# Coupled outputs of four batches taken ahead, x1 parts moved to the coupling's third cycle, and a new order at the last batch

## The reference

```python
xn = layernorm(x)
# attention and feed-forward branch
q, k, v = split(xn @ Wqkv + bqkv); qp, kp = elu(q) + 1, elu(k) + 1
attn = qp @ (kp^T v) / (qp . sum(kp) + eps)
x1 = layer_norm(xn + attn) * g1 + b1
ffn = (silu(x1 @ Wg + bg) * (x1 @ Wu + bu)) @ Wd + bd        # 341 hidden features
s = layer_norm(x1 + ffn) * g2 + b2
# coupling branch
gf = global_net(mean(xn)); out = xn
for _ in range(3):
    tf = sigmoid(gelu(gelu(gelu(out @ w1 + b1) @ w2 + b2) @ w3 + b3) @ w4 + b4)     # one number a token
    out = out + (0.1 + range * 2 * (0.7 * gf + 0.3 * tf - 0.5)) * twist(out)
result = x + s * silu(out)
```

## Time and profile before

| | us |
|---|---|
| median of 3 runs | 187.56 |
| profiled execution, whole | 185.62 |
| its span, first to last instruction | 183.8 |
| TensorE busy (matmul) | 161.3 |
| VectorE busy | 146.4 |
| ScalarE busy | 124.9 |
| GpSimd busy | 107.9 |

### The profile page before, as it was taken

The page is one execution under the profiler, slowest core; times in us unless marked ns, Lnnn a source line. Parts: engine busy times, 40 slices in busy tenths (PEclk is TensorE's granted clock), DMA queues, the critical chain, the costliest instruction groups (busy, mean ns, idle before and its releaser), DMA issues.

```text
span 183.8 us, 3473 instructions
## 1 busy us (share of the span) xinstructions
PE 161.3 (88%) x979; PEld 114.0 (62%) x982; DVE 146.4 (80%) x567; ACT 124.9 (68%) x320; POOL 107.9 (59%) x204
## 2 busy tenths in 40 slices
PE   0289999999999989989969899789999999999920
PEld 0146777777777776446524445448887887888820
DVE  4694789999987988599999940366969889889695
ACT  2227866988979976978856685885576765774430
POOL 0259667879994689950011223139768586595981
PEclk9999999999999999999997999999999999999996
DMA  5980000000000000000000000000001010010113
GB/s 98 312 338 0 0 0 5 0 2 2 0 4 0 2 5 0 0 4 0 0 0 0 2 4 0 2 0 4 2 0 57 0 61 32 27 57 4 59 57 114
DMA packets 3331, 5.75 MB, mean 31 GB/s; under 512 B 496, under 2 KB 1136, under 8 KB 3312
## 3 DMA queue, kind: packets, MB, share of 16 engines
q1 hardware_dynamic: 3312, 5.52, 9.0%
HBM read 3.43 MB, written 2.10 MB: 30 GB/s over the span
## 4 chain that ended last, share of the span: by engine, by line
PE 54%; DVE 21%; POOL 8%; ACT 7%; issue 4%; DMA 3%; SPq 1%; DVEq 0%; ACTq 0%; POOLq 0%
PE bank L1041 11%; DVE r_tok L639 6%; PE bank L1029 6%; PE bank L1030 5%; PE bank L1031 5%; DVE pq L652 5%; PE bank L885 5%; DVE r_tok L642 3%; DMA r_tok<-in_w_first 3%; POOL rstd L231 3%; PE bank L969 3%; PE bank L918 2%; PE bank L919 2%; PE bank L921 2%; PE bank L930 2%
## 5 line engine op out<-in xcount | busy, mean ns | idle before, releaser
L441 ACT ACTIVATE pq<-bank,bffn 128x512 f32<-128x512 f32 (+1 forms) x24 | 16.3, 685 | 16.4 <-PE bank L1031 16.4
L231 POOL TENSOR_TENSOR rstd<-ve,minus_half 128x4 f32<-128x4 f32 (+1 forms) x25 | 24.8, 992 | 2.1
L1041 PE MATMUL bank<-wd,pq 128*128 128x128 f32 x168 | 23.4, 283 | 0.0
L230 POOL TENSOR_SCALAR ve<-mv 128x4 f32<-128x4 f32 (+1 forms) x25 | 5.1, 206 | 30.1 <-DVE nm L539 29.2
L1029 PE MATMUL bank<-x_hi,ffn_hi 128*128 128x512 f32 (+1 forms) x48 | 20.8, 433 | 1.8 <-ACT pq L441 1.3
L676 DVE SCALAR_TENSOR_TENSOR pq<-bank,bffn,pq 128x512 f32<-128x512 f32 (+1 forms) x24 | 17.8, 746 | 5.0 <-ACT pq L441 3.2
L1041 PEld LDWEIGHTS bank<-wd,pq 128*128 128x128 f32 x168 | 21.2, 193 | 0.2
L392 ACT ACTIVATE q_stage<-bank,col 128x512 f32<-128x512 f32 x24 | 16.3, 686 | 6.8 <-PE bank L885 6.0
L1030 PE MATMUL bank<-x_lo,ffn_hi 128*128 128x512 f32 (+1 forms) x48 | 19.0, 396 | 0.0
L1031 PE MATMUL bank<-x_hi,ffn_lo 128*128 128x512 f32 (+1 forms) x48 | 19.0, 395 | 0.0
L921 PE MATMUL bank<-first_hi,xT_lo 128*128 128x512 f32 x32 | 15.4, 482 | 0.0
(11 more groups left out here) (134 smaller groups left out, 463.6 us busy)
## 6 DMA issues: line engine op xcount, KB each, us to landing
x_tok<-in_x SPq DMA_DIRECT2D x8, 256.0 KB, 6.3
out<-pq SPq DMA_DIRECT2D x7, 256.0 KB, 2.0
r_tok<-in_w_ffn SPq DMA_DIRECT2D x1, 341.0 KB, 6.2
r_tok<-in_w_first SPq DMA_DIRECT2D x1, 320.0 KB, 5.3
out<-pq SPq DMA_DIRECT2D x2, 128.0 KB, 1.8
small<-in_w_small SPq DMA_DIRECT2D x1, 242.0 KB, 4.0
row<-in_rows SPq DMA_DIRECT2D x1, 192.0 KB, 5.8
wd<-in_w_down SPq DMA_DIRECT2D x1, 192.0 KB, 6.3
```

Of the source, the lines that this page charges most:

```text
L231: return pool.tensor_tensor(rstd[i][:, b, ts], ve[i][:, b, ts], minus_half[:, ts], ALU.pow)
L1041: last = pe.matmul(dst[:, t * P:(t + 1) * P], hid[b % 2][0:m, c, t * P:(t + 1) * P], wd[0:m, c], start=False, stop=(c == CHUNKS - 1))
```

## The change

- **Coupled outputs.** For batches 0 to 3 (`EARLY`) GpSimd, not ScalarE, computes `a * xn`, in place in SBUF, directly behind the scalars of a pair; VectorE adds `b * twist` from there in slots 10 and 11, ahead of the first hidden product. Batches 4 to 7 stay on ScalarE, with a semaphore of their own, and are spread over the first batches of the feed-forward.
- **Late x1 parts.** Transposition and high part of batches 6 and 7 move from slots 2 and 4 to slots 8 and 9, their low parts on VectorE from slots 1 and 3 to behind the updates of slot 7 and the coupling of slot 8. The multiplications by g1 of these batches move behind all scalars on GpSimd.
- **Third chunk.** Gate and up products of chunk 2 go to banks 1 and 2, which the coupling's layer 2 has left, and wait for no SiLU or hidden product.
- **SiLU of chunk 0** moves ahead of the last tanh on ScalarE.
- **Last batch's order.** The whole down product of batch 6 stands between chunks 22 and 23 on TensorE, and VectorE takes the residual of batch 6 ahead of hidden product 23.

```diff
@@ -34,6 +34,8 @@
 CHUNKS = -(-HID // P)
 CHUNK_ROWS = [min(P, HID - c * P) for c in range(CHUNKS)]
 ACT_NORMS = 5
+EARLY = 4
+X1_SLOTS = {0: 5, 8: 6, 9: 7}
 PAIRS = BATCHES // 2
 CYCLES = 3
 HALVES = ((0, 1), (2, 3))
@@ -180,12 +182,18 @@
         ctx_ready, gf_ps, gf_act, base_ready = sem("ctx_ready"), sem("gf_ps"), sem("gf_act"), sem("base_ready")
         h1_ps, h1_ready, h2_ps, h2_ready = sem("h1_ps"), sem("h1_ready"), sem("h2_ps"), sem("h2_ready")
         h3_ps, h3_ready, z_ps, tt_ready = sem("h3_ps"), sem("h3_ready"), sem("z_ps"), sem("tt_ready")
-        r_ready, s_ready, cpl_ready, ab_ready, ax_ready, o_ready = [
-            sem(n) for n in ("r_ready", "s_ready", "cpl_ready", "ab_ready", "ax_ready", "o_ready")]
+        r_ready, s_ready, cpl_ready, ab_ready, ax_ready, axp_ready, o_ready = [
+            sem(n) for n in ("r_ready", "s_ready", "cpl_ready", "ab_ready", "ax_ready", "axp_ready", "o_ready")]
         gate_ps, up_ps, sg_ready, hid_ready = sem("gate_ps"), sem("up_ps"), sem("sg_ready"), sem("hid_ready")
         down_ps, u2_ready, un_ready = sem("down_ps"), sem("u2_ready"), sem("un_ready")
         g_ready, mn_ready, y_ready = sem("g_ready"), sem("mn_ready"), sem("y_ready")
         y_stored = [sem("y_stored0"), sem("y_stored1")]
+
+        def gate_of(n):
+            return bank[1] if n == 2 else ps_gate[n % 2]
+
+        def up_of(n):
+            return bank[2] if n == 2 else ps_up[n % 2]
         block = ctx.enter_context(nc.Block())
@@ -293,6 +301,13 @@
                 pool.tensor_tensor(a, a1, t1, ALU.subtract)
                 pool.tensor_tensor(b, b1, t0, ALU.add).then_inc(ab_ready, 1)
+            def scale_xn(b):
+
+                pool.wait_ge(ab_ready, b // 2 + 1)
+                pool.wait_ge(tx_ready, b + 1)
+                a = ab[:, b // 2, 2, TILES * (b % 2):TILES * (b % 2) + TILES].unsqueeze(2).to_broadcast([P, TILES, D])
+                pool.tensor_tensor(xn_tok[:, b], xn_tok[:, b], a, ALU.mult).then_inc(ax_ready, 1)
+
             def gate_rows(b):
                 pool.wait_ge(g_ready, b + 1)
@@ -318,12 +333,15 @@
                     norm_x1(b - 2)
                 if 3 <= b < BATCHES + 1:
                     scale_x1(b - 3)
-            for b in (BATCHES - 2, BATCHES - 1):
-                scale_x1(b)
             for j in range(PAIRS):
                 scalars_2(j)
             for j in range(PAIRS):
                 scalars_3(j)
+                if 2 * j < EARLY:
+                    scale_xn(2 * j)
+                    scale_xn(2 * j + 1)
+            for b in (BATCHES - 2, BATCHES - 1):
+                scale_x1(b)
             for b in range(BATCHES):
                 gate_rows(b)
                 if b == BATCHES - 1:
@@ -417,14 +435,14 @@
             def scale_xn(b):
                 act.wait_ge(ab_ready, b // 2 + 1)
-                if b == 0:
+                if b == EARLY:
                     act.wait_ge(tt_ready, SLOTS)
                 else:
                     act.wait_ge(o_ready, b)
                 for t in range(TILES):
                     i = TILES * (b % 2) + t
                     last = act.mul(ps_ax[:, t], xn_tok[:, b, t], ab[:, b // 2, 2, i:i + 1])
-                last.then_inc(ax_ready, 1)
+                last.then_inc(axp_ready, 1)
             def silu_o(b):
                 act.wait_ge(o_ready, b + 1)
@@ -438,7 +456,7 @@
                 if n == 0:
                     act.wait_ge(bffn_ready, 1)
                 m = CHUNK_ROWS[c]
-                act.activation(sg[n % 2][0:m], ps_gate[n % 2][0:m], ACT.Silu,
+                act.activation(sg[n % 2][0:m], gate_of(n)[0:m], ACT.Silu,
                                bias=bffn[0:m, c:c + 1]).then_inc(sg_ready, 1)
             def norm_2(b):
@@ -477,8 +495,8 @@
             global_act(2)
             for s in range(SLOTS - 2):
                 gelu_2(s)
-                if s in (0, 2, 4):
-                    hi_x1(BATCHES - 3 + s // 2)
+                if s in X1_SLOTS:
+                    hi_x1(X1_SLOTS[s])
                 if s >= 1:
                     tanh_z(s - 1)
                 gelu_1(s + 2, (0,))
@@ -490,16 +508,16 @@
             gelu_3(SLOTS - 2)
             tanh_z(SLOTS - 2)
             gelu_3(SLOTS - 1)
+            silu_gate(0)
             tanh_z(SLOTS - 1)
             for b in range(BATCHES + 1):
                 if b < BATCHES:
-                    silu_gate(CHUNKS * b)
-                    if b == 0:
-                        scale_xn(0)
+                    if b >= 1:
+                        silu_gate(CHUNKS * b)
                     silu_gate(CHUNKS * b + 1)
-                    if b + 1 < BATCHES:
-                        scale_xn(b + 1)
                     silu_gate(CHUNKS * b + 2)
+                if EARLY <= b + EARLY < BATCHES:
+                    scale_xn(b + EARLY)
                 if b == 0:
                     silu_o(0)
                 if b >= 2:
@@ -657,11 +675,15 @@
             def o3(b):
                 j = b // 2
-                dve.wait_ge(ax_ready, b + 1)
+                if b < EARLY:
+                    dve.wait_ge(ax_ready, b + 1)
+                else:
+                    dve.wait_ge(axp_ready, b - EARLY + 1)
                 for t in range(TILES):
                     i = TILES * (b % 2) + t
                     last = dve.scalar_tensor_tensor(out=xn_tok[:, b, t], in0=tx_tok[:, b, t],
-                                                    scalar=ab[:, j, 3, i:i + 1], in1=ps_ax[:, t],
+                                                    scalar=ab[:, j, 3, i:i + 1],
+                                                    in1=xn_tok[:, b, t] if b < EARLY else ps_ax[:, t],
                                                     op0=ALU.mult, op1=ALU.add)
                 last.then_inc(o_ready, 1)
@@ -673,7 +695,7 @@
                 dve.wait_ge(sg_ready, n + 1)
                 if b >= 2:
                     dve.wait_ge(down_ps, b - 1)
-                dve.scalar_tensor_tensor(out=hid[b % 2][0:m, c], in0=ps_up[n % 2][0:m],
+                dve.scalar_tensor_tensor(out=hid[b % 2][0:m, c], in0=up_of(n)[0:m],
                                          scalar=bffn[0:m, CHUNKS + c:CHUNKS + c + 1], in1=sg[n % 2][0:m],
                                          op0=ALU.add, op1=ALU.mult).then_inc(hid_ready, 1)
@@ -847,21 +869,26 @@
                     next_r(s)
                 if 2 <= s < PAIRS + 2:
                     minus_s(s - 2)
-                if s in (1, 3):
-                    lo_x1(BATCHES - 2 + s // 2)
+                if s in (7, 8):
+                    lo_x1(s - 1)
+                if s >= SLOTS - 2:
+                    o3(2 * (s - SLOTS + 2))
+                    o3(2 * (s - SLOTS + 2) + 1)
             for b in range(BATCHES):
                 hidden(CHUNKS * b)
                 if b >= 3:
                     finish(b - 3)
-                if b == 0:
-                    o3(0)
                 hidden(CHUNKS * b + 1)
-                if b + 1 < BATCHES:
-                    o3(b + 1)
+                if b + EARLY < BATCHES and b >= 1:
+                    o3(b + EARLY - 1)
+                if b == BATCHES - 1:
+                    residual_2(b - 1)
                 hidden(CHUNKS * b + 2)
-                if b >= 1:
+                if 1 <= b < BATCHES - 1:
                     residual_2(b - 1)
+                if b == BATCHES - EARLY:
+                    o3(BATCHES - 1)
             last = BATCHES - 1
             residual_last(0)
@@ -1019,16 +1046,16 @@
             def gate_up(n, parts=(0, 1)):
                 b, c = divmod(n, CHUNKS)
                 m = CHUNK_ROWS[c]
-                if n >= 2 and 0 in parts:
+                if n >= 3 and 0 in parts:
                     pe.wait_ge(sg_ready, n - 1)
                 for k in parts:
-                    dst, done = ((ps_gate, gate_ps), (ps_up, up_ps))[k]
-                    if k == 1 and n >= 2:
+                    dst, done = ((gate_of(n), gate_ps), (up_of(n), up_ps))[k]
+                    if k == 1 and n >= 3:
                         pe.wait_ge(hid_ready, n - 1)
                     w = slice(k * HID + c * P, k * HID + c * P + m)
-                    pe.matmul(dst[n % 2][0:m], ffn_hi[:, w], x1_hi[:, b], start=True, stop=False)
-                    pe.matmul(dst[n % 2][0:m], ffn_hi[:, w], x1_lo[:, b], start=False, stop=False)
-                    pe.matmul(dst[n % 2][0:m], ffn_lo[:, w], x1_hi[:, b], start=False, stop=True).then_inc(done, 1)
+                    pe.matmul(dst[0:m], ffn_hi[:, w], x1_hi[:, b], start=True, stop=False)
+                    pe.matmul(dst[0:m], ffn_hi[:, w], x1_lo[:, b], start=False, stop=False)
+                    pe.matmul(dst[0:m], ffn_lo[:, w], x1_hi[:, b], start=False, stop=True).then_inc(done, 1)
             def down(b, tiles):
                 pe.wait_ge(hid_ready, CHUNKS * (b + 1))
@@ -1103,8 +1130,8 @@
                 if s == 1:
                     pe.wait_ge(gf_act, 3)
                 layer_2(s)
-                if s in (0, 2, 4):
```

(16 more changed lines are left out.)

## The result

| | before | changed |
|---|---|---|
| median of the runs, us | 187.23 (184.88 to 188.20, 4 runs) | 191.94 (191.62 to 193.08, 4 runs) |
| profiled execution, us | 185.62 | 191.97 |
| its span, us | 183.8 | 190.2 |
| mean granted clock | 0.983 | 0.959 |

The change made the kernel slower: 1.0314 times the time before [1.0245 to 1.0384, the 95% interval], and 4.7 us in the medians; the forecast for the median was 191.4. The two profiled executions are 6.35 us apart, and that splits into four stretches, of which one lies in code that the change does not touch.

What follows compares the result with a forecast made beforehand. TensorE binds from 123 to 173 us, VectorE's update chain before that; +1.1 (early outputs, coupling included), +1.5 (clock), +1.3 (last batch) make +3.9 us, median 191.4, own range 189.8 to 192.9, overall 188.0 to 193.3.

Steps and rivals of the forecast that it cites:

- The coupling: Coupling slots up to layer 1 behind slot 9: of VectorE's 1.8 us lead only 0.09 us is left.
- the wait in slot 9: TensorE in slot 9 stands 1.17 us, its moved transposition of batch 7 waiting for batch 6's low part.
- The early outputs: Feed-forward entry: first hidden product at 121.5 instead of 117.76, first down product at 125.05 instead of 123.95, +1.1 us.
- The hold of batch 3's: Ahead of the first hidden product, GpSimd's g1 multiplications hold batch 3's first two VectorE updates, 1.30 us each instead of 0.27.
- Rival A: Ahead of the first hidden product GpSimd waits, not VectorE; 187.9 to 189.4 us; chance 0.21.
- The clock: Behind TensorE's 4.3 us standing at the fourth up product, the clock falls: +1.5 us, bounds 0 and 2.5.
- The last batch: At the end, batch 5's normalisation behind the last SiLU delays GpSimd's finish and the last stores: +1.3 us.
- Sum: Whole kernel: +1.1 + 1.5 + 1.3 = +3.9 us on the profiled 185.62, giving 189.5; median 191.4.
- B: Faster: VectorE's lead reaches TensorE, placed at slot 9; 185.4, up to 186.8 us; chance 0.18.
- C: Clock falls a second time, behind the 1.17 us standing in slot 9: +1.5 more, 192.9 us; chance 0.07.
- D: Tanh needs its own table: two loads more, 1.28 us each, before slot 11's coupling or second gate; 192.7 to 194; chance 0.03.

Runs made afterwards that it cites:

- hidden-first experiment: Changed kernel with VectorE's updates of batches 2 and 3 moved from ahead of the first hidden product to behind the third: 191.96 us, 1.0287.
- the second execution: Both kernels profiled once more, unchanged: 186.79 us for the kernel before, 192.67 us for the changed kernel.
- the two experiments: Changed kernel with the last batch's old order: 190.41 us, 1.0209; kernel before with only the last batch's new order: 187.94 us, 1.0053.

## Why the prediction was right, and where its terms were off

**The coupling** was right: forecast -0.09, measured -0.20, with the wait in slot 9 at 1.23 us for a forecast 1.17. The experiment that removed it shows it worth 1.27 us.

**The early outputs** were forecast at +1.1, the coupling's gain included, and took 0.62 (0.82 without that gain). The first hidden product came at 122.53, less the front 120.90, for a forecast 121.5. One step of it failed: I priced GpSimd's scaling at 1.31 us per batch from the earlier trace rows, a multiplication by a row, and this one multiplies by a scalar per tile and took 2.04 / 2 = 1.02. So the first pair's updates were not held; only the coupling ahead of them was, by 0.30 us, and the hidden product came 0.6 us sooner than forecast. The hold of batch 3's was as forecast, 2.05 us for 2.06. The Trainium skill, "SBUF — State Buffer", section "SBUF: two separate sides", calls the shared pair an exclusive lock that the first comer keeps; 2.18 against 4.23 us agrees, and so do the 9.44 us of the hidden-first experiment.

**Rival A**, that GpSimd waits and not VectorE, is out as a size: its multiplications took 1.26 to 1.37 us with an update waiting and 1.27 with none. A GpSimd operation that waits for an update is seen only in the small scalars, 0.25 us at 115.87 beside the updates for 0.20 elsewhere.

**The clock** was the mis-sized term: +1.5 forecast, bounds 0 and 2.5, and 2.77 measured, over the upper bound; the second execution lost 2.57 (131.20 - 124.92 - 3.71), the kernels with the old last batch and with the earlier low part 1.54 and 1.55. I had taken the loss from a fall in the coupling that lasted 3.75 us. Where the fall was as short, about 3.4 us, the price was right; in the changed kernel it lasted from about 123.2 to 130.0.

**The last batch**: forecast +1.3, measured 1.36 in the trace, 1.0 and 1.5 by the two experiments.

**Sum.** +3.9 forecast; +4.7 without the front. Entry and clock erred in opposite directions (-0.5, +1.3), and it is partly luck that the sum came as close as it did. The median, 191.94, is 0.5 over the forecast. The front was in no term; that the profiled execution before was 1.94 us under the median I carried over as it was, and about 1.2 of it is the fall at 68 us, if the second execution is typical: the first happened not to have it. Had the base been taken without that difference, 189.5 would have been 2.4 us too low.

**The other rivals.** B failed as a whole because the wait in slot 9 and the hold were both real, but its place was well chosen: with either removed the kernel gains 2.7 to 3.9 us, the clock's part included. C did not happen where it was placed: behind the standing in slot 9 (0.97 to 1.23 us in the seven executions that had it) the granted clock was 1.00 from 107 to 115 us. A fall earlier in the coupling, about slots 7 and 8, came in one of the changed kernel's two executions, at half its price (0.7 us). D is out: no load between the SiLU at 117.34 and the tanh at 117.93. The Trainium skill, "ScalarE: Activation LUTs", section "Table sets: the hidden batching unit", names sets that hold tanh and none with SiLU; in the trace tanh ran between two SiLUs with no load, so the set loaded for SiLU served it too.

## What to carry to other kernels

Ask of a step that is moved what the other of GpSimd and VectorE does at its new place, not only whether its own engine has room: the same eight updates cost 2.2, 4.2 or 9.4 us by that alone. Where an engine that binds the rest stands for several microseconds, price the clock behind it apart from the wait, and widely. A package of edits can hide a good one: the first pair early and the second pair late made the kernel 1.3% faster where both early made it 3.1% slower.

## What was not expected of the hardware

- GpSimd's multiplication of 128x512 by one number per token of each tile took 1.02 us, by a row 1.27 to 1.31 us.
- Eight VectorE updates beside an unbroken row of GpSimd multiplications took 9.44 us, one let through per multiplication; GpSimd's own were hardly longer (1.26 to 1.37).
- After 3.65 us of standing the loss to the low clock was 2.77, 2.57, 1.55 and 1.54 us in four executions: more where it fell before TensorE started again, less where it fell after.
- The clock can fall at 68 us in the kernel before in one execution and not in another, at a cost of 1.57 us; the two spans differ by 1.2.
